# Build of a count matrix in a graph kernel: the reads of the bucketed edges paced by the hits, the marks' scatters between them

## What is computed

```python
h = jnp.maximum(_layernorm(x, axis=-1), 0.0)
x = x + _L0_gnn_ref(h, edge_index, ...)          # agg = segment_sum(h[src], dst)
x = x + _L1_gnn_ref(h1, edge_index, ...)         # softmax over incoming edges, weighted sum of (h1 @ W)[src]
x = x + _L2_gnn_ref(h2, edge_index, ...)         # three times: mean over neighbours @ Wl + h @ Wr + b
x = x + _L3_gnn_ref(h3, edge_index, edge_attr_64, ...)
# in L3: h = relu([h3[row], edge_attr] @ W1a + b1a) @ W1b + b1b, mean over col, then an MLP on [h3, agg, u]
```

## Time and profile before

| | |
|---|---|
| median of three runs | 9022.21 us |
| span of the profiled execution, first to last instruction | 9030.2 us |
| build of the matrix, about | 2446 to 3640 us |
| edge pass, first part, about | 6921 to 8730 us |
| mean granted TensorE clock | 0.837 |

### The profile page before, as it was taken

One profiled execution on the slowest core, in us unless ns is written; L12 is line 12 of the kernel. 1 busy time (PEld: TensorE's weight loads), 2 busy tenths in 40 slices (PEclk: granted clock), 3 DMA queues, 4 the chain that ended last, 5 costly groups with the idle time before them and its releaser, 6 DMA issues. The chain is left out here.

```text
span 9030.2 us, 137943 instructions
## 1 busy us (share of the span) xinstructions
PE 6296.6 (70%) x36507; PEld 4249.3 (47%) x36507; DVE 6360.5 (70%) x17765; ACT 2836.5 (31%) x6169; POOL 2691.6 (30%) x2966
## 2 busy tenths in 40 slices
PE   4767777777555666566501788599997777777779
PEld 3545555555312222222201777444445666666668
DVE  6777777777668999655588999611024777777778
ACT  0222222222245776344400788300001333320000
POOL 0666767766646200000000000000002444444430
PEclk9666666666667999799855999799999999999999
DMA  2333333333498555699597666276676776752256
GB/s 98 94 96 95 97 97 97 96 97 97 127 393 270 163 169 145 227 337 329 163 387 311 207 215 213 95 245 217 215 251 178 180 183 179 181 144 63 63 105 194
DMA packets 1048196, 1605.78 MB, mean 178 GB/s; under 512 B 111567, under 2 KB 699236, under 8 KB 1033906
## 3 DMA queue, kind: packets, MB, share of 16 engines
q1 hardware_dynamic: 761756, 1179.89, 41.4%
q0 software_dynamic: 111328, 277.62, 9.5%
q10 hardware_dynamic: 174394, 139.51, 5.8%
HBM read 1177.49 MB, written 419.08 MB: 177 GB/s over the span
## 5 line engine op out<-in xcount | busy, mean ns | idle before, releaser
L774 POOL DMA_INDIRECT bucketed<-arena,wide x1563 | 1527.1, 977 | 882.6 <-issue 850.6
L2161 PE MATMUL psum<-wide,arena 128*128 x6496 | 1210.4, 329 | 397.5 <-DVE arena L2220 391.5
L2161 PEld LDWEIGHTS psum<-wide,arena 128*128 128x128 f32 x6496 | 989.2, 195 | 616.9 <-issue 491.8
L2220 DVE TENSOR_SCALAR arena<-wide,tile_first 128x128 f32 x3248 | 871.4, 302 | 469.4 <-PE psum L2161 289.8
L2082 POOL DMA_INDIRECT arena<-table,src_i x832 | 802.0, 964 | 1006.9 <-PE psum L2178 870.8
L942 PE MATMUL psum<-arena 128*128 128x512 bf16 x2304 | 705.8, 444 | 425.5 <-DVE arena L890 247.4
L662 PE MATMUL psum<-w_edge,arena 128*128 128x256 f32 x1568 | 869.7, 655 | 0.0
L890 DVE TENSOR_SCALAR arena<-sums 128x512 bf16<-128x512 int16 x2304 | 821.1, 356 | 0.0
L691 ACT CAST wide<-psum 49x49 f16<-49x49 f32 x1568 | 310.8, 198 | 1556.0 <-PE psum L669 893.9
L2030 POOL DMA_DIRECT2D table<-wide x13 | 9.6, 736 | 2478.5 <-DVE wide L1929 2478.5
L1686 PE MATMUL psum<-sums,arena 128*128 128x129 f32 x4802 | 602.3, 281 | 154.3 <-DVE arena L1676 154.3
(11 more groups left out here) (475 smaller groups left out, 12384.7 us busy)
## 6 DMA issues: line engine op xcount, KB each, us to landing
arena<-halved SPq DMA_DIRECT2D x441, 384.0 KB
arena<-adjacency SPq DMA_DIRECT2D x98, 1568.0 KB, 7.8
adjacency<-wide SPq DMA_DIRECT2D x588, 256.0 KB, 2.3
arena<-adjacency SPq DMA_DIRECT2D x196, 640.0 KB, 3.9
arena<-adjacency SPq DMA_DIRECT2D x147, 768.0 KB, 6.8
arena<-bucketed POOLq DMA_DIRECT2D x208, 528.0 KB, 6.1
halved<-arena SPq DMA_DIRECT2D x147, 384.0 KB, 6.3
wide<-bucketed ACTq DMA_DIRECT2D x208, 256.0 KB
```

What stands on the lines that cost most here:

```text
L774: e.indirect_dma_start(bucketed, bass.IndirectOffsetOnAxis(ap=places[k][0:size, c:c + 1], axis=0), rows[k][0:size, c, :], None).then_inc(s ...
L2161: e.matmul(flat[:, ds((chunk & 3) * 512 + 2048, P)], lhsT=hot[:, i % 8, :], rhs=table_in[:, ds(tile * P, P)], start=False, stop=True, skip ...
L2220: e.tensor_scalar(hot[:, i % 8, :], rows[:, ds((chunk[k] & 15) * P, P)], tile_first[:, ds(tile[k], 1)], None, op0=ALU.is_equal).then_inc(l ...
```

## The change

- The reads of POOL in the build are no longer issued as soon as a buffer is free. Before the copy of read n, where n + 4 is the first read of a block of 16, POOL waits until `s_found` has passed the block two before it (`AHEAD = 2`).
- The 49 pairs of indirect DMAs for the marks stand between the reads now: one pair after every four reads, in the first 49 of 52 turns. The wait for the marks' blank fill stands ahead of the first copy.
- Each wait on a register's value goes through `at_least_zero`, which ands the value with 4095. It stands in five places: TensorE's and ScalarE's waits in the build, ScalarE's and VectorE's in the edge pass. All values are between 1 and 4095, so none changes.

```diff
+AHEAD = 2
...
+def at_least_zero(value, bits=4095):
+    return value & bits
...
+                    def mark(b):
+                        e.indirect_dma_start(look_marks, bass.IndirectOffsetOnAxis(ap=look_to[:, b:b + 1], axis=0),
+                                             look_code[:, b:b + 1], None).then_inc(s_look_mark, 16)
+                        e.indirect_dma_start(chunk_marks, bass.IndirectOffsetOnAxis(ap=chunk_to[:, b:b + 1], axis=0),
+                                             chunk_code[:, b:b + 1], None).then_inc(s_chunk_mark, 16)
                     def one(i, more=True):
                         for k in range(LOADS):
                             n = LOADS * i + k
+                            ahead = (n + LOADS) * BODY // P - AHEAD
+                            if more and ahead >= 0 and (n + LOADS) * BODY % P == 0:
+                                e.wait_ge(s_found, ahead + 1)
                             e.wait_ge(s_ring[k], 16 * i + 16)
...
-                    rounds_of(ROUNDS // LOADS - 1, one)
-                    one(ROUNDS // LOADS - 1, False)
+                    e.wait_ge(s_marks, 32)
+                    for i in range(ROUNDS // LOADS):
+                        one(i, i < ROUNDS // LOADS - 1)
+                        for b in range(i, TILES, ROUNDS // LOADS):
+                            mark(b)
...
-                    e.wait_ge(s_marks, 32)
-                    for b in range(TILES):
-                        e.indirect_dma_start(look_marks, ...)
-                        e.indirect_dma_start(chunk_marks, ...)
...
-                                    e.wait_ge(s_clear, bucket[k + BANKS - 1])
+                                    e.wait_ge(s_clear, at_least_zero(bucket[k + BANKS - 1]))
...
-                                e.wait_ge(s_used, end[g])
+                                e.wait_ge(s_used, at_least_zero(end[g]))
...
-                        e.wait_ge(s_looked, end)
+                        e.wait_ge(s_looked, at_least_zero(end))
...
-                                e.wait_ge(s_clear, chunk[k + 1])
+                                e.wait_ge(s_clear, at_least_zero(chunk[k + 1]))
```

More of the change, by code:

```diff
@@ L62 @@
 SLOPE = 0.2
+assert max(HITS + RUN, LOOKS, NEAR + 16) <= 4095
 assert NEAR % (4 * QUAD) == 0 and FAR_PAIRS * PER_PAIR >= LOOKS and LOOKS % PER_PAIR == 0 and MARKS < DUMP
```

## The result

The changed kernel takes 9058.40 us, median of five runs (9051.78 to 9069.86); the kernel before took 9031.19 beside it. The medians lie 27 us apart. The ratio, in which all runs of both kernels count, is 1.0036, 95% interval 1.0023 to 1.0049: slower, by some 33 us, where 9011 and a small gain were forecast. The profiled execution spans 9055.0 us, 24.8 more than before.

A forecast was written before the change was run, and what follows sets the result against it. VectorE was taken to bound the build, slowed by late stores while reads ran. Build -51 us (66 gained, 15 lost at the start) and edge pass +40 gave 9011 us against the median; range 8943 to 9078, the forecast's own 8975 to 9055.

The forecast's parts named there:

- The stage's bound and its chain: Build: VectorE bounds it undisturbed; during reads, slow stores hold ScalarE, then TensorE, then VectorE, costing 0.69 us a read.
- the pace: Build: reads wait for the finding of block c-2, binding only from block 4; costed at nothing.
- (c): Edge pass: VectorE's sequencer becomes the bound, 0.22 us a pair or more, pass +90 or more; 9072, chance 0.16.
- (d): Build: contention is conserved, 0.69 us a read wherever it stands; +55 in all, 9077, chance 0.11.
- What they do now is thin the reads ... 0.34 us a read: Build: scatters between reads leave stores at 86%, so 190 reads lose 65 us in place of 131, 66 gained.
- the 1.34 us of engines for a read: Build: DMA time one read takes of all 16 engines, from 73.6% of 300 us over 165 reads.
- (a): Build: reads thin out further, 0.10 us a read, with 20 us lost in the edge pass; 8945, chance 0.12.
- The start: Build: scatters delay the first hit by about 7 us and the second transposition by 8, 15 us lost together.
- The edge pass: Register operations cost VectorE 0.32 us a pair of chunks, most of it covered; 0.10 a pair counts, +40 us.
- what hides them is TensorE: Edge pass: VectorE goes from 3.90 to 4.22 us a pair, level with TensorE's 4.17, which covers most of the cost.
- (b): Register operations are hidden: edge pass 0, build -51; 8971, chance 0.13.
- (e): Build: the pace does not bind because POOL is later than the hits; near the forecast, chance 0.05 with the rest.

The follow-up runs named there:

- an even pace: Changed kernel with reads released one by two by the hits multiplied, in place of sixteen at a block's finding: 1.0016 of the kernel before.
- seven buffers: Seven staging buffers for the count matrix in place of four: 0.9951 in the changed kernel, 0.9943 with even pace and fewer VectorE waits, against the kernel before.
- the second and: Changed kernel with another and (with 2047) behind the first in VectorE's edge-pass wait: 1.0116 of the kernel before.

## Why the prediction was wrong

**The stage's bound and its chain** were read rightly, and so was the pace: it binds from block 4, no block is over 73 after the first, and the blocks stand nearer to the 62 of the forecast than to 90, at 66. That the measured time lies inside 8943 to 9078 at all is owed to the rivals (c) and (d), for whose sake the range was that wide; the forecast's own range ended at 9055.

**"What they do now is thin the reads ... 0.34 us a read" is the step that failed.** The pair of scatters does stretch the turn, to 9.3 us and to 9.0 without the pace (9.5 forecast), but the stores did not run at 86% beside it. Without the pace they ran at 71%, and a read cost 0.66 us; in the changed kernel it cost 0.60, not 0.34. Of the 66 us that the thinner reads were to gain, some 27 came: the build's 14.9 and the 12 that the later start took.

The term that was too small is the 1.34 us of engines for a read, taken as fixed. It was 1.48 with the marks between and no pace, and 0.383 x 580 / 143 = 1.55 in the changed kernel. With 1.05 in all and 0.655 for the reads, the same balance leaves the stores 0.39 of 0.58, 67%. The marks' own packets are not the difference: they are under 1% of the engines' time in that stretch. The packets of the reads, 4224 bytes each, have a median of 164 ns in every stretch, and only their mean goes up: 167 ns before, 183 with the marks between and no pace, 193 in the changed kernel, 221 at an even pace. Why some take longer stays open.

And a balance of mean shares would have been wrong even with the right term. Over the changed kernel's stretch the mean share is 0.86 of 1.06, room for everything, and a read costs 0.60; at an even pace its packets take 1.80 us and it costs 0.49; with seven buffers 1.74 and 0.20. What set the price where the engines have gaps is how long a late store leaves ScalarE without a buffer, as the runs with seven buffers show. The prediction listed the four banks' slack as what speaks for rival (a); there was little. With the pace and no scatters between the reads the build was the same, so the pace is enough for all of the gain.

**The start** was right: first hit 5.1 us later after the first read (7 forecast), and the second transposition's wait 48.3 - 34.3 = 14.0 us instead of 7.3 (8 forecast). The block with the whole-array operations took 16 us over 56.4, as the 15 us before.

**The edge pass** failed only in size. VectorE's best pair went from 3.90 to 4.19 (4.22 forecast), level with TensorE's 4.17; of the 0.29 us, 0.136 came through, not 0.10, which makes +55 in place of +40. The late mean, 4.40, lies between the 4.33 of the forecast and the 4.45 of rival (c). Its reasoning, that level engines don't catch up a delay, fits the second and, which cost 0.25 on the mean and 0.29 late. That "what hides them is TensorE" was too simple: VectorE had 0.27 us a pair in hand at its best, and still about half of 0.29 came through. TensorE waited for VectorE about once a pair before the change already; that this is where the rest was lost is argued, not tested.

**The rivals.** (b) is refuted, and with it the use I made there of the Trainium skill (Advanced Engine Details and Errata, Sequencer Loop and Engine Queue Depths): register operations between short instructions were not hidden by a queue, since the sequencer itself set the pace. (c) needed 0.22 a pair and got 0.136. (d), contention conserved at 0.69 a read, was nearest: 0.66 with the marks between alone, 0.60 with the pace. It had the build 15 us longer, though, and it was 15 us shorter. The kernel ended slower as the build gained 15 in place of 51, against an edge pass of +55; with 51 the two would about cancel. (e) is out, POOL waited 242.1 us at the new wait. On the Trainium skill's rule (SBUF — State Buffer, SBUF: two separate sides), the trace agrees in part: the median read's issue went from 528 to 700 ns in the changed kernel's stretch, where VectorE is busy 503 of 580 us in place of 186 of 300. It had no price to be seen, as POOL waited 242.1 us at the pace anyway.

## What to carry to other kernels

Pacing a background load helps little without buffers deep enough for the foreground's latency: here either alone was worth 8 to 21 us, both 74. Read the price of contention from the wait chain (who stands without a buffer, how long a transfer takes to land), not from the balance of mean shares. And before adding a register operation to a loop of short instructions, compare the best pace of that engine with its partner's: what is left between them is the most that can hide it. Here it was 0.27 us a pair, and hid half of 0.29.

## What the runs showed that I had not expected

In the run with the ands only, one block of hits took 164.1 us while POOL issued the marks' scatters. From 3421 to 3547 us TensorE's sequencer ran at a small part of its speed. Its register operations at the hits, first from 3430 to 3535 us, then undisturbed from 3700 to 3800 (ns min/median/max):

```profile
L947 PEldq ALU_OP  x30: 688/700/1395, 3430.8 to 3533.1; - x30
...
L947 PEldq ALU_OP  x224: 32/32/32, 3701.3 to 3798.8; - x112
```

700 ns in place of 32, and 30 hits took 105 us, where 224 took 98 us undisturbed. It ended by itself, 14 us after the last scatter was issued. The other runs of that kernel took 9639 to 9708 us, 56 to 125 less than the profiled one, so the disturbance comes and goes.

Is it the scatters behind the last read? The other kernels that leave them there show no such block in their traces. The one with the pace alone has four slow ones between 3745 and 3756 us, though, of some 640 ns, and three of its twelve runs took 50 to 100 us over its median, as if they had the long case; no trace of them was kept. The kernel with the marks between and no pace, beside it, had no run more than 13 us over its median. Against the scatters as the cause stands the slow pair at the start of the edge pass, with the same 700 ns in the eight traces of the slower chips and in none of the faster: the marks' scatters are long done there. POOL issues other indirect DMAs in those microseconds, but it does so on the faster chip too. The cause stays open.
